# Cross attention and int4 FFN on one core: plain fp32 scores and skip for the first three batches, a new run-in order, and a first FFN that takes both halves per weight pair

## What is computed

```python
def reference(x, ctx_1024, Wq, Wk, Wv, Wskip, qweight, scales, zeros, bias):
    x = x + xattn(_layernorm(x), ctx_1024, Wq, Wk, Wv, Wskip)
    x = x + ffn(_layernorm(x), qweight, scales, zeros, bias)
    return x
def xattn(up, down, Wq, Wk, Wv, Wskip):
    q = einsum('oc,bcn->bon', Wq, up)
    k, v = einsum('oc,bcm->bom', Wk, down), einsum('oc,bcm->bom', Wv, down)
    attention = softmax(einsum('bcn,bcm->bnm', q, k) / sqrt(128), axis=-1)
    return einsum('oc,bcn->bon', Wskip, up) + einsum('bnm,bcm->bcn', attention, v)
def ffn(x, qweight, scales, zeros, bias):
    low, high = qweight & 15, qweight >> 4 & 15
    w = (interleave(low, high) - round(zeros / scales).T) * scales.T
    return einsum('bsi,io->bso', x, w) + bias
```

## Time and profile before

| | us |
|---|---|
| median of 3 runs | 525.16 (524.19 to 525.29) |
| the profiled execution, its own time | 524.91 |
| its span, first to last instruction | 522.7 |
| what lies around the span | 2.2 |
| TensorE busy | 497.4 (95%) |
| GpSimd busy | 470.2 (90%) |
| VectorE busy | 428.0 (82%) |
| ScalarE busy | 372.8 (71%) |
| mean granted TensorE clock | 0.987 of full |

### The profile page before, as it was taken

One profiled execution on the slowest core, in us unless ns is written; L12 is line 12 of the kernel. 1 busy time (PEld: TensorE's weight loads), 2 busy tenths in 40 slices (PEclk: granted clock), 3 DMA queues, 4 the chain that ended last, 5 costly groups with the idle time before them and its releaser, 6 DMA issues.

```text
span 522.7 us, 9248 instructions
## 1 busy us (share of the span) xinstructions
PE 497.4 (95%) x2653; PEld 304.3 (58%) x2685; DVE 428.0 (82%) x983; ACT 372.8 (71%) x844; POOL 470.2 (90%) x717
## 2 busy tenths in 40 slices
PE   4659999999999999999999999999999999999997
PEld 3545665656666565666656566665656666565544
DVE  6899888889888888988888898888889888887652
ACT  4978877777877777787777778777776877777520
POOL 4899899999999999999999999999999999999753
PEclk9788999999999999999999999999999999999999
DMA  8636787797698789878887987989787698756764
GB/s 314 179 79 136 149 207 184 184 195 184 169 190 193 178 179 194 184 181 189 189 176 178 191 184 180 187 198 170 181 188 188 171 188 195 172 131 140 164 125 123
DMA packets 227203, 92.65 MB, mean 177 GB/s; under 512 B 209488, under 2 KB 214352, under 8 KB 227152
## 3 DMA queue, kind: packets, MB, share of 16 engines
q1 hardware_dynamic: 226432, 91.91, 76.7%
q10 hardware_dynamic: 720, 0.14, 0.1%
HBM read 23.87 MB, written 16.78 MB: 78 GB/s over the span
## 4 chain that ended last, share of the span: by engine, by line
PE 81%; POOL 6%; DVE 5%; DMA 3%; ACT 2%; issue 2%; SPq 0%; POOLq 0%; ACTq 0%
PE ps_y L940 38%; PE ps_e L905 15%; PE ps_o L935 14%; PE ps_o L931 7%; PE ps_kv L916 3%; PE ps_kv L918 2%; POOL sb_prob L262 1%; PE ps_y L944 1%; DMA sb_pt_lo<-sb_p_lo 1%; DMA sb_xnt_lo<-sb_xn_lo 1%; POOL sb_xc_lo L277 1%; ACT sb_prob L485 1%; DMA sb_x<-in_x_dram 1%; DVE sb_st L601 1%; DVE sb_neg_max L664 1%
## 5 line engine op out<-in xcount | busy, mean ns | idle before, releaser
L940 PE MATMUL ps_y<-sb_wf,sb_xnt_hi 128*128 128x512 f16 x496 | 188.3, 380 | 4.0 <-DMA sb_xnt_lo<-sb_xn_lo 1.4
L940 PE MATMUL ps_y<-sb_wf,sb_xnt_lo 128*128 128x512 f16 x496 | 188.0, 379 | 0.0
L485 ACT ACTIVATE sb_prob<-ps_e,sb_neg_max 128x256 f32<-128x256 f32 x256 | 118.3, 470 | 58.9 <-DVE sb_neg_max L664 58.9
L262 POOL TENSOR_SCALAR sb_prob<-sb_prob,sb_rsum 128x256 f32<-128x256 f32 x256 | 122.4, 491 | 15.3 <-DVE sb_rsum L669 14.9
L673 DVE TENSOR_TENSOR sb_p_lo<-sb_prob,sb_p_hi 128x1024 f16<-128x1024 f32 x64 | 78.1, 1221 | 49.1 <-ACT sb_p_hi L494 49.1
L905 PE MATMUL ps_e<-sb_k_hi,sb_xc_hi 128*128 128x256 f32 x256 | 90.6, 354 | 8.7 <-DVE sb_k_lo L652 5.7
L256 POOL TENSOR_TENSOR sb_o<-sb_prod,sb_x 128x512 f32<-128x512 f32 x63 | 80.2, 1273 | 5.8 <-DVE sb_prod L707 5.8
L664 DVE TENSOR_REDUCE sb_neg_max<-ps_e 128x2 f32<-128x512 f32 x128 | 84.8, 682 | 0.5
L940 PEld LDWEIGHTS ps_y<-sb_wf,sb_xnt_hi 128*128 128x128 f16 x496 | 48.5, 98 | 59.9 <-DMA sb_xnt_lo<-sb_xn_lo 2.3
L940 PEld LDWEIGHTS ps_y<-sb_wf,sb_xnt_lo 128*128 128x128 f16 x496 | 48.5, 98 | 54.7
L494 ACT ACTIVATE sb_p_hi<-sb_prob 128x1024 f16<-128x1024 f32 x64 | 67.3, 1052 | 18.1 <-issue 15.2
(11 more groups left out here) (137 smaller groups left out, 929.2 us busy)
## 6 DMA issues: line engine op xcount, KB each, us to landing
sb_x<-in_x_dram SPq DMA_DIRECT2D x32, 512.0 KB, 4.0
out_dram<-sb_o SPq DMA_DIRECT2D x63, 256.0 KB, 2.4
sb_ctx<-in_ctx_dram SPq DMA_DIRECT2D x32, 128.0 KB, 2.7
sb_q<-in_L_ffn_qweight_dram SPq DMA_DIRECT2D x4, 512.0 KB, 7.7
sb_pt_hi<-sb_p_hi SPq DMA_TRANSPOSE x64, 3.0
sb_pt_lo<-sb_p_lo SPq DMA_TRANSPOSE x64, 2.8
sb_scale_row<-in_L_ffn_scales_dram SPq DMA_DIRECT2D x1, 512.0 KB, 9.9
sb_xnt_hi<-sb_xn_hi SPq DMA_TRANSPOSE x32, 2.8
```

The source lines that it names most:

```text
L262: last = pool.tensor_scalar(prob[:, j, t, :], prob[:, j, t, :], rsum[:, j, t:t + 1], P_SCALE, ALU.mult, ALU.mult)
L485: done = act.activation(prob[:, j, t, :], ps_e[j % 2][:, t, :], ACT.Exp, bias=neg_max[:, j, t:t + 1], accum_out=esum[:, j, t:t + 1])
L940: pe.matmul(ps_y[h][:, :], xnt_p[s][:, q % 2, kt, :], wf[:, kt, h * HALF:(h + 1) * HALF], start=kt == 0 and s == 0, stop=False)
```

## The change

The change has four parts.

1. For batches 0 to 2 (`WHOLE` = 3) the centred x, the keys and the skip weights stay whole in float32 (`x_whole`, `k_whole`, `wsk_whole`): no `centred_hi`, `centred_lo`, `keys_lo`, `wsk_lo`, and one plain float32 matmul where three split products stood, in `scores` and in the skip.
2. All five run-ins are new and one batch longer: they hold the scores of batch 2, the attention of batch 1, the whole weight preparation and the first FFN, and `run_steps` begins at step 3. `skip_attend` is cut into `skip` and `attend`, and `turn_xn` into its two halves.
3. `first_ffn` takes both output halves for each pair of weight tiles and ends both at the end, where `ffn(0, 0)` and `ffn(0, 1)` took one half after the other.
4. The rows for the seed use bank `ps_y[1]` in place of `ps_y[0]`.

Steps 3 and later are the same on each engine, but for the skip of batch 2.

```diff
     P = nc.NUM_PARTITIONS
     HALF = 512
     QUARTER = 256
+    WHOLE = 3
...
             def run_in():
                 sp.wait_ge(kv_done, 1)
                 load_ctx(2)
                 load_x(3)
                 turn_probs(0, 0)
-                turn_probs(0, 1)
                 sp.wait_ge(kv_done, 2)
                 load_ctx(3)
-                turn_probs(1, 0)
+                turn_probs(0, 1)
                 sp.wait_ge(kv_done, 3)
                 load_ctx(4)
+                turn_probs(1, 0)
                 sp.wait_ge(x1_done[1], 1)
                 load_x(4)
                 turn_probs(1, 1)
-                turn_xn(0)
+                turn_xn_hi(0)
+                turn_xn_lo(0)
 
             run_in()
             run_steps(step, 2)
...
@@ -371,24 +381,32 @@
                 inverse_std1(1)
                 normalise(0, 0)
                 normalise(0, 1)
-                centred_lo(1, 0)
                 normalise(0, 2)
-                centred_lo(1, 1)
                 normalise(0, 3)
                 zero_point_remainder()
                 inverse_std1(2)
                 normalise(1, 0)
-                centred_lo(2, 0)
                 normalise(1, 1)
-                centred_lo(2, 1)
-                zero_point_rounding()
-                inverse_std1(3)
                 normalise(1, 2)
                 normalise(1, 3)
+                zero_point_rounding()
+                zero_point_sign()
+                normalise(2, 0)
                 inverse_std2(0)
                 seed_sources()
+                normalise(2, 1)
                 split_row_sum(0)
                 xn_low(0)
+                normalise(2, 2)
+                normalise(2, 3)
+                inverse_std1(3)
+                inverse_std2(1)
+                centred_lo(3, 0)
+                centred_lo(3, 1)
+                inverse_std1(4)
+                write_out(0, 0)
+                split_row_sum(1)
+                xn_low(1)
...
             def centre(n):
                 act.wait_ge(mv1_done, n + 1)
-                if ran(n, 1):
-                    act.wait_ge(xclo_done, HALVES * n)
-                act.activation(xc[:, :], x_sb[:, n % 4, :], ACT.Identity, bias=mv1[:, 0:1],
-                               scale=-1.0).then_inc(xc_done, 1)
+                if n > WHOLE:
+                    act.wait_ge(xclo_done, HALVES * (n - WHOLE))
+                act.activation(xc[:, :] if n >= WHOLE else x_whole[:, n, :], x_sb[:, n % 4, :],
+                               ACT.Identity, bias=mv1[:, 0:1], scale=-1.0).then_inc(xc_done, 1)
 
             def centred_hi(n):
                 act.wait_ge(xc_done, n + 1)
-                if ran(n, 3):
+                if n >= WHOLE + 3:
                     act.wait_ge(attn_done[1], n - 2)
                 act.activation(xc_hi[:, n % 3, :], xc[:, :], ACT.Copy).then_inc(xchi_done, 1)
...
             def run_in():
                 centre(0)
-                first_centred_hi(0)
                 keys_hi(0)
-                first_centred_hi(1)
                 keep_projections()
                 centre(1)
                 exps(0, 0)
                 exps(0, 1)
                 keys_hi(1)
-                centred_hi(1)
+                values_hi(0)
                 exps(0, 2)
+                exps(0, 3)
                 probs_hi(0, 0)
-                exps(0, 3)
-                values_hi(0)
+                probs_hi(0, 1)
                 exps(1, 0)
-                probs_hi(0, 1)
                 centre(2)
                 exps(1, 1)
-                centred_hi(2)
                 values_hi(1)
-                unpack(0)
                 exps(1, 2)
+                exps(1, 3)
                 probs_hi(1, 0)
-                exps(1, 3)
-                unpack(1)
                 keys_hi(2)
+                probs_hi(1, 1)
                 values_hi(2)
-                probs_hi(1, 1)
+                exps(2, 0)
+                exps(2, 1)
+                exps(2, 2)
+                exps(2, 3)
                 apply_norm2(0)
                 xn_high(0)
+                unpack(0)
+                probs_hi(2, 0)
+                unpack(1)
+                unpack(2)
+                probs_hi(2, 1)
+                unpack(3)
+                centre(3)
+                keys_hi(3)
+                values_hi(3)
+                centred_hi(3)
+                apply_norm2(1)
+                xn_high(1)
...
             def values_lo(n):
                 dve.wait_ge(kvhi_done, n + 1)
-                dve.scalar_tensor_tensor(wsk_lo[:, n % 3, :], proj[:, SKIP, :], sk_scale[:, :],
-                                         wsk_hi[:, n % 3, :].bitcast(F32), ALU.mult, ALU.subtract)
+                if n >= WHOLE:
+                    dve.scalar_tensor_tensor(wsk_lo[:, n % 3, :], proj[:, SKIP, :], sk_scale[:, :],
+                                             wsk_hi[:, n % 3, :].bitcast(F32), ALU.mult, ALU.subtract)
...
             def run_in():
                 stats1(0, 0)
@@ -751,9 +758,6 @@
                 keep_key()
                 context_max(0)
                 scale_weights()
-                first_centred_lo(0)
-                keys_lo(0)
-                first_centred_lo(1)
...
+                row_max(0, 2)
                 invert(0, 1)
-                keys_lo(1)
-                row_max(0, 2)
                 row_max(0, 3)
+                values_lo(0)
                 invert(0, 2)
                 stats1(2, 0)
+                row_max(1, 0)
+                invert(0, 3)
+                stats1(2, 1)
                 probs_lo(0, 0)
-                invert(0, 3)
-                row_max(1, 0)
-                stats1(2, 1)
                 aggregate1(2)
-                values_lo(0)
+                probs_lo(0, 1)
                 variance1(2)
                 row_max(1, 1)
-                probs_lo(0, 1)
                 invert(1, 0)
                 value_scale(1)
-                nibbles(0)
-                residual(0, 0)
+                row_max(1, 2)
                 invert(1, 1)
                 context_max(2)
+                row_max(1, 3)
                 values_lo(1)
-                row_max(1, 2)
-                row_max(1, 3)
+                residual(0, 0)
+                invert(1, 2)
+                invert(1, 3)
+                value_scale(2)
+                probs_lo(1, 0)
+                residual(0, 1)
+                row_max(2, 0)
+                probs_lo(1, 1)
+                row_max(2, 1)
+                row_max(2, 2)
+                invert(2, 0)
                 stats2(0, 0)
+                stats2(0, 1)
+                aggregate2(0)
+                invert(2, 1)
+                row_max(2, 3)
+                values_lo(2)
+                context_max(3)
+                residual(1, 0)
+                residual(1, 1)
+                nibbles(0)
+                invert(2, 2)
+                invert(2, 3)
                 nibbles(1)
-                invert(1, 2)
+                seed_rows()
+                probs_lo(2, 0)
+                nibbles(2)
                 stats1(3, 0)
                 stats1(3, 1)
                 aggregate1(3)
                 variance1(3)
-                value_scale(2)
-                residual(0, 1)
-                probs_lo(1, 0)
-                invert(1, 3)
-                stats2(0, 1)
-                aggregate2(0)
-                keys_lo(2)
-                values_lo(2)
-                context_max(3)
-                nibbles(2)
-                probs_lo(1, 1)
+                nibbles(3)
+                probs_lo(2, 1)
+                value_scale(3)
+                stats2(1, 0)
+                stats2(1, 1)
+                aggregate2(1)
+                keys_lo(3)
+                values_lo(3)
+                context_max(4)
+                stats1(4, 0)
+                stats1(4, 1)
+                aggregate1(4)
+                variance1(4)
+                scale_product(0, 0)
...
             def scores(b, j):
-                if j == 0:
-                    pe.wait_ge(klo_done, b + 1)
-                if j % (CHUNKS // HALVES) == 0:
-                    pe.wait_ge(xclo_done, HALVES * b + 1 + j // (CHUNKS // HALVES))
+                if b < WHOLE:
+                    if j == 0:
+                        pe.wait_ge(xc_done, b + 1)
+                        pe.wait_ge(khi_done, b + 1)
+                else:
+                    if j == 0:
+                        pe.wait_ge(klo_done, b - WHOLE + 1)
+                    if j % (CHUNKS // HALVES) == 0:
+                        pe.wait_ge(xclo_done, HALVES * (b - WHOLE) + 1 + j // (CHUNKS // HALVES))
...
+                    if b < WHOLE:
+                        last = pe.matmul(ps_e[j % 2][:, t, :], x_whole[:, b, cols],
+                                         k_whole[:, b, :], start=True, stop=True)
+                        continue
...
-            def skip_attend(a, h):
+            def skip(a, h):
                 cols = slice(h * HALF, (h + 1) * HALF)
```

(39 more changed lines are left out.)

76 lines of the change are left out of this document (28 added, 48 removed).

## The result

| kernel | median us | lowest to highest | ratio to before, 95% interval |
|---|---|---|---|
| before | 525.03 (5 runs) | 524.19 to 525.29 | |
| after | 527.26 (5 runs) | 526.31 to 528.22 | 1.0046 [1.0035, 1.0057] |

The change makes the kernel slower by 0.46%, 2.2 us. The forecast was slower, by 5.3 us (530.4). The profiled execution of the changed kernel took 528.22, span 526.2; the one of before 524.91, span 522.7.

The account below looks back on a forecast made before the run. TensorE, busy for 95% of the span, was taken as the bound, with 465.4 us that only slide after batch 3's scores start. Losses of 4.1 + 0.35 + 0.8 = 5.3 us gave 530.4, range 525.0 to 532.8.

Parts of the forecast that it names:

- Prices: Per operation: plain tile 0.44 us against 0.35 split; GpSimd held 0.88 by a probs_lo, 0.96 by a nibbles.
- Steps 1 and 2: Run-in to exps(1,0): batch 1's scores at 16.2, 0.9 us earlier; then exps(1,0) at 21.0, 1.1 lost.
- Step 3: TensorE at half clock after over 3 us idle, in batch 1's scores and skip; residual(0,0) at 28.0, 2.0 us lost.
- Step 4: From residual(0,0) to GpSimd's inverse_std2(0), with one hold of 0.88 us: it starts at 38.1, 1.25 lost.
- Step 5: GpSimd from inverse_std2(0) to the end of xn_low(0): work 7.4 us, holds 3.8; ends at 49.3, 3.3 lost.
- Step 6: Queue and transpose from xn_low(0) to the first FFN take 2.9 us; the FFN starts at 52.3.
- Step 7: First FFN: 3.8 us at half clock after idling cost 1.9; it takes 9.1, batch 3's scores at 61.4, 4.1 lost.
- Step 8: Losses after batch 3's scores start: 0.35 us for batch 2's plain skip, 0.8 for new waits; second FFN just covered.
- the clock stays up: Rival: TensorE keeps 2.4 GHz in batch 1's work and recovers at once in the first FFN: 527.4 us; chance 0.12.
- The hold is the whole instruction: Rival: VectorE holds GpSimd for entire instructions, six holds 0.35 us longer each: 532.5 us; chance 0.14.
- The holds miss the chain: Rival: GpSimd works in gaps between VectorE's holds; without all six, 524.0 us; decides from 4.4 us missed; chance 0.12.
- It comes out even: Rival: four of six holds missed, or run-in waits absorb the rest: 525.2 us; chance 0.10.

Follow-up runs that it names:

- sections 2 and 6: 2: changed kernel with nibbles(0) and nibbles(1) earlier on VectorE, 526.07 us; 6: changed kernel with load_x(4) behind turn_probs(1,1), 528.08 us.
- section 3: Changed kernel with six unused matmuls ahead of the first FFN, 528.32 us; with nibbles(0) and nibbles(1) also early, 525.84 us.
- `stats2` early: Changed kernel with batch 0's second normalisation moved ahead on VectorE, GpSimd and ScalarE: 527.85 us, ratio 1.0060.
- `warm` alone: Changed kernel with six plain fp32 matmuls that nothing uses ahead of first_ffn on TensorE: 528.32 us, ratio 1.0071.

## Why the prediction was right in sign and wrong in size

By its own steps, in the profiled execution, where the sum was made.

- **Bound.** Right to 0.75 us: after 60.05 the rest slides. From batch 3's scores to the end it is 466.15 us, against 465.4.
- **Prices.** Right. The plain tile takes 0.43 (four in 1.73 from 32.06 to 33.79), I took 0.44. A pair of nibbles costs 0.89 to 1.0 of GpSimd (sections 2 and 6), a `probs_lo` 0.97; I took 0.96 and 0.88.
- **Steps 1 and 2.** Order right, each about 1 late: batch 1's scores at 17.04 (16.2), `exps(1,0)` at 22.05 (21.0). Of that 0.38 is the launch (the first matmul at 5.32, before 4.94).
- **Step 3.** Right in the sum, in part by luck: an idle stretch of 3.55, then half clock, but about 1 us later than I had it. `scores(1,2)` takes 1.06 (forecast 1.8), the skip 1.70 (1.7), `scores(1,3)` 1.62 (0.9), together 4.38 (4.4), and `residual(0,0)` comes at 28.99 (28.0).
- **Step 4.** `inverse_std2(0)` at 39.13 (38.1): no new error, the 1.0 carried on.
- **Step 5 failed.** It reads: "VectorE's list puts `nibbles(0)`, `nibbles(1)`, `probs_lo(2,0)` and `nibbles(2)` beside it: 3 x 0.96 + 0.88 = 3.8." The work is the 7.4 it said (7.27 measured with the nibbles away), but only the first two hold anything on the way: 1.77. The span is 9.04 and not 11.2, 2.2 us too much in the forecast. The reason is the place of `nibbles(0)`, which I had let follow VectorE's own work, and which really waits for `residual(1,1)`, so for `attend(1,1)`, so for a transpose that shares the DMA engines with the load of x(4). The trace of the run with that load moved shows the forecast's case but for the last hold, which falls on VectorE there, and the run with the nibbles away shows the price. So the mechanism was right, and the number of holds on the way hung on a wait of 1.6 us that I had not followed.
- **Step 6.** 2.98 measured, 3.0 between the forecast's starts (2.9 by its rows).
- **Step 7.** The numbers nearly fit (FFN 8.9 long, I said 9.1; 3.4 us at half clock, I said 3.8; idle for 6.89 ahead of it, I said some 8), the reason does not: the half clock is no term of the sum. Without it, batch 3 waits for ScalarE (section 3); it becomes one only when the nibbles are out of the way, as in section 2's trace. The step says of the weights that "these come in time in the change"; it didn't ask when `xc_lo` of batch 3 comes, which waits for the same engine.
- **Step 8.** 1.15 forecast. From batch 3 to the third FFN after takes 24.74 us and before 23.34, so 1.40 more: 0.35 for the plain skip, and waits of 0.49 and 0.26 ahead of the second and third FFN are named in it. By the end of the span 0.65 of it has come back, 0.75 is left; where it comes back I did not trace.

Sum in the profile: forecast 530.2, measured 528.22. The 2.0 are 1.35 at batch 3 (2.2 and 0.2 too much in steps 5 and 7, 1.0 too little in 1 to 4), 0.4 in step 8 and 0.2 around the span. The other 1.2 us between 530.4 and 527.26 lie between profile and median: I carried over the 0.25 of the kernel before, and this kernel's profiled executions are 1.0 above their median, twice. Why is open.

What the sum hid: it set the plain operands' cost against their saving and looked only at where batch 3 starts. Each part was worth more than the total: -4.1 and +6.6.

The rivals: "the clock stays up" would have been 527.4, near the result for a reason that the traces exclude, as the clock did fall. "The hold is the whole instruction" is out by the prices. "The holds miss the chain" happened in part, 2.0 of the 4.4 us that it needs to decide. "It comes out even" is out: the two intervals of after begin at 1.0035 and 1.0036.

## What to carry to other kernels

A chain that ends a stage is not enough: list every wait of the instruction that starts the next stage, and follow each to its start. Here two chains on different engines ended less than 0.2 us apart, and shortening one by 2.9 us gave nothing. When a change bundles new operands with a new order, price them apart before adding them up; the plain operands were worth taking alone. A hold between two engines is worth its price only where both instructions really meet, and that place has to be worked out from waits, not from the order of a list.

## What the runs showed of the hardware

- **The hold goes both ways.** In the run of `stats2` early, `nibbles(0)` meets `xn_low(0)`: its two instructions take 1.14 and 1.64 instead of 0.68 and 0.69, while `xn_low` is only 0.43 longer. In the run with the late load `probs_lo` takes 1.77 instead of 1.22 beside `xn_low`. I had counted the loss on GpSimd alone. The Trainium skill, "SBUF — State Buffer", section "SBUF: two separate sides", says that the one that issues first gets the port pair and the other blocks; the traces agree that either can lose. The Trainium skill says in the same place that the pair is held for the whole instruction; here a pair of nibbles, 1.2 us from start to start, costs GpSimd 0.89 to 1.0.
- **A transpose beside a load.** The DMA issue of `probs_lo(1,1)` takes 2.48 us and `attend(1,1)` waits for it while a 512 KB load runs; with the load behind it 1.31. (The transpose of `probs_hi(1,1)` just ahead of it takes 1.24 and 1.23, with the load and without.) The load's own issue then takes 2.09 and not 0.58.
- **The launch varies by a microsecond.** The first matmul lies between 4.94 and 5.64 in all these traces, the weight transposes between 8.0 and 9.6, and half clock can fall in the first scores (8 matmuls in 3.62) or not (2.63). Later waits take such a delay back in part or not at all: with the load late the transposes are 0.6 behind those of after and `inverse_std2(0)` 0.2; with `warm` alone they are 0.9 behind and the first FFN still 1.0. A difference of a microsecond between two single traces can be this.
